# Probabilities times keys in three rounded passes, the high half kept by ScalarE and the low half by VectorE

## What is computed

```python
x = _layernorm(x + attention(x))                  # linear: A = sum(l2norm(K) * V); Y = A * l2norm(Q)
x = _layernorm(x + cross_attention(ctx, x))       # below
x = _layernorm(x + experts(x))                    # 8 experts, the best 2 of each row

def cross_attention(image, latents):              # image = ctx, latents = x; 16 heads of width 64
    kv_in = concat([norm(image), norm(latents)])  # 128 rows of keys per sequence
    w = softmax((norm(latents) @ Wq) * (kv_in @ Wk) / 8)
    return (w @ (kv_in @ Wv)) @ Wo
```

## Time and profile before

| | us |
|---|---|
| median of three runs | 1611.88 (1607.72 to 1613.25) |
| the profiled execution, whole | 1606.26 |
| its span, first to last instruction | 1604.4 |
| TensorE busy | 1432.5 (89%) |
| VectorE busy | 1105.5 (69%) |
| ScalarE busy | 1031.7 (64%) |
| GpSimd busy | 904.7 (56%) |

### The profile page before, as it was taken

One profiled execution on the slowest core, in us unless ns is written; L12 is line 12 of the kernel. 1 busy time (PEld: TensorE's weight loads), 2 busy tenths in 40 slices (PEclk: granted clock), 3 DMA queues, 4 the chain that ended last, 5 costly groups with the idle time before them and its releaser, 6 DMA issues.

```text
span 1604.4 us, 36488 instructions
## 1 busy us (share of the span) xinstructions
PE 1432.5 (89%) x10509; PEld 1239.7 (77%) x10509; DVE 1105.5 (69%) x4107; ACT 1031.7 (64%) x3827; POOL 904.7 (56%) x1233
## 2 busy tenths in 40 slices
PE   5699999999999999999999999999997499999940
PEld 4578888888888888888888888888886498889940
DVE  3366777767777677776777767777666588777865
ACT  2377776777767777677776777767764255555535
POOL 3355556665566665666556665566544255455565
PEclk9799999999999999999999999999999699999975
DMA  2000000000000000000000000000000676677746
GB/s 78 11 11 8 15 16 15 18 16 15 16 15 18 17 14 16 15 18 17 14 16 15 17 17 14 16 16 17 10 10 14 181 242 218 213 221 225 222 153 196
DMA packets 64624, 96.18 MB, mean 60 GB/s; under 512 B 10892, under 2 KB 48786, under 8 KB 64306
## 3 DMA queue, kind: packets, MB, share of 16 engines
q1 hardware_dynamic: 44738, 71.90, 15.0%
q0 software_dynamic: 8896, 16.94, 3.1%
q10 hardware_dynamic: 10800, 5.06, 1.2%
HBM read 71.55 MB, written 23.35 MB: 59 GB/s over the span
## 4 chain that ended last, share of the span: by engine, by line
PE 69%; DVE 10%; ACT 9%; DMA 4%; issue 4%; POOL 2%; SPq 2%; ACTq 0%; POOLq 0%; DVEq 0%
PE ps_s L1208 15%; PE ps_o L1221 11%; PE ps_t L1241 10%; ACT probs L607 6%; PE ps_pT L1231 5%; PE ps_t L1371 3%; PE ps_u L1256 3%; PE ps_a L1307 3%; PE ps_u L1258 3%; PE ps_u L1257 3%; DVE neg_max L759 3%; DVE pT L771 3%; PE ps_u L1371 2%; DVE k_pick L814 2%; DMA f_x<-x_rows 2%
## 5 line engine op out<-in xcount | busy, mean ns | idle before, releaser
L607 ACT ACTIVATE probs<-ps_s,neg_max 128x128 f32<-128x128 f32 x1024 | 361.8, 366 | 290.2 <-DVE neg_max L759 290.2
L496 POOL TENSOR_TENSOR probs_n<-probs,inv_sum 128x512 f32<-128x512 f32 x256 | 265.9, 1039 | 251.6 <-DVE inv_sum L765 249.6
L1208 PE MATMUL ps_s<-kvT,u_sb 128*128 128x128 f32 x2048 | 281.1, 280 | 0.0
L1208 PEld LDWEIGHTS ps_s<-kvT,u_sb 128*128 128x128 f32 x2048 | 255.2, 192 | 33.2 <-issue 31.8
L1241 PE MATMUL ps_t<-pT,kv_rows 128*128 128x512 f32 x512 | 262.2, 594 | 0.8 <-DVE pT L771 0.8
L1221 PE MATMUL ps_o<-value_w,tT 128*128 128x128 f32 x2048 | 260.5, 275 | 2.4 <-ACT tT L618 2.2
L759 DVE TENSOR_REDUCE neg_max<-ps_s 128x4 f32<-128x512 f32 x256 | 176.2, 688 | 103.9 <-PE ps_s L1208 103.4
L1221 PEld LDWEIGHTS ps_o<-value_w,tT 128*128 128x128 f32 x2048 | 244.0, 192 | 4.3 <-ACT tT L618 4.3
L553 POOL DMA_INDIRECT y_rows<-wvT,f_id x144 | 144.8, 1006 | 152.4 <-DVE wvT L1118 94.9
L607 ACT ACTIVATION_READ_ACCUMULATOR probs<-ps_s,neg_max 128x1 f32 x1024 | 208.2, 203 | 0.0
L508 POOL DMA_INDIRECT x_rows<-routed,pos_i x128 | 136.7, 1068 | 121.2 <-DVE pos_i L950 101.0
(11 more groups left out here) (237 smaller groups left out, 3165.6 us busy)
## 6 DMA issues: line engine op xcount, KB each, us to landing
u_sb<-in_expert_w SPq DMA_DIRECT2D x45, 578.0 KB
tT<-in_expert_w SPq DMA_DIRECT2D x27, 578.0 KB
f_x<-x_rows SPq DMA_DIRECT2D x72, 130.0 KB
tT<-y_rows SPq DMA_DIRECT2D x16, 512.0 KB, 4.7
x_raw<-in_x SPq DMA_DIRECT2D x64, 64.0 KB, 1.8
c_raw<-in_ctx_in SPq DMA_DIRECT2D x64, 64.0 KB, 2.0
out<-u_sb ACTq DMA_DIRECT2D x16, 256.0 KB, 2.4
y_rows<-wvT,f_id POOLq DMA_INDIRECT x144
```

The costliest lines, as they stand in the source:

```text
L496: nc.gpsimd.tensor_tensor(probs_n[:, sl], probs[:, sl], inv_sum[:, sl, :].rearrange("p (u o) -> p u o", o=1).to_broadcast([P, UP, P]), ALU ...
L607: last = nc.scalar.activation(probs[:, sl, j], ps_s[sl][:, j * P:(j + 1) * P], ACT.Exp, bias=neg_max[:, sl, j:j + 1], accum_out=sums[:, sl ...
L1208: last = nc.tensor.matmul(ps_s[sl][:, j * P:(j + 1) * P], u_sb[:, c // 2, BT * p + b, h:h + 2].rearrange("p h s -> p (h s)"), kvT[:, c, 2 ...
```

## The change

The key rows and the transposed probabilities are each kept as a rounded high half and the float32r rest: kv_hi, kv_lo, pT_hi, pT_lo. weigh becomes three rounded passes of 512 columns into the same bank: high x high, low x high, high x low; the third waits for pT_lo. ScalarE writes pT_hi (`round_pT`, behind the copy of u in each unit) and kv_hi; VectorE writes pT_lo = ps_pT - pT_hi (`keep_pT`, now of unit n-2, directly behind row_max(n)) and kv_lo (`rows_low`, in unit 2). turn_probs waits for pT_lo_done in place of pT_done, and at k = 1 and 3 stands behind latents_part in place of ahead of it; two small products wait for kv_lo_done in place of kv_done.

```diff
-        kv_rows = sb("kv_rows", [P, KV_RING, BT, D])
+        kv_hi = sb("kv_hi", [P, KV_RING, BT, D], F32R)
+        kv_lo = sb("kv_lo", [P, KV_RING, BT, D], F32R)
...
-        pT = sb("pT", [P, 2, UP * P])
+        pT_hi = sb("pT_hi", [P, 2, UP * P], F32R)
+        pT_lo = sb("pT_lo", [P, 2, UP * P], F32R)
...
+            def round_pT(t, k):
+                m, ss = t * 4 + (k - 1), (k - 1) % 2
+                act.wait_ge(pT_ps, m + 1)
+                act.wait_ge(t_ps, count(m - 1))
+                nc.scalar.activation(pT_hi[:, ss], ps_pT[:], ACT.Copy).then_inc(pT_hi_done, 1)
...
                         nc.scalar.activation(u_sb[...], ps_u[...], ACT.Copy).then_inc(u_done, 1)
+                    if unit_on(t, k - 1):
+                        round_pT(t, k)
...
-                        nc.scalar.activation(kv_rows[:, (t + 2) % KV_RING], KV_BACK..., ACT.Copy).then_inc(kv_done, 1)
+                        nc.scalar.activation(kv_hi[:, (t + 2) % KV_RING], KV_BACK..., ACT.Copy).then_inc(kv_hi_done, 1)
...
                 def keep_pT(k):
-                    m, ss = t * 4 + (k - 1), (k - 1) % 2
-                    dve.wait_ge(pT_ps, m + 1)
-                    dve.wait_ge(t_ps, count(m - 1))
-                    nc.vector.tensor_copy(pT[:, ss], ps_pT[:]).then_inc(pT_done, 1)
+                    m, ss = t * 4 + (k - 2), k % 2
+                    dve.wait_ge(pT_hi_done, m + 1)
+                    nc.vector.tensor_tensor(pT_lo[:, ss], ps_pT[:], pT_hi[:, ss].bitcast(F32), ALU.subtract).then_inc(pT_lo_done, 1)
...
+                def rows_low():
+                    dve.wait_ge(kv_hi_done, t + 3)
+                    nc.vector.tensor_tensor(kv_lo[...], KV_BACK..., kv_hi[...].bitcast(F32), ALU.subtract).then_inc(kv_lo_done, 1)
...
                 if on(t, 0):
                     row_max(0)
+                if unit_on(t, -2):
+                    keep_pT(0)
...
                 if on(t, 0):
                     inverse_sum(0)
-                if unit_on(t, -1):
-                    keep_pT(0)
...
                 if on(t, 0):
                     row_max(2)
+                if unit_on(t, 0):
+                    keep_pT(2)
+                if on(t, 2):
+                    rows_low()
...
             def turn_probs(t, k):
-                pe.wait_ge(pT_done, m)
+                pe.wait_ge(pT_lo_done, m)
...
             def weigh(t, k, p):
-                pe.wait_ge(pT_done, m + 1)
-                pe.wait_ge(kv_done, m // 4 + 1)
+                pe.wait_ge(pT_hi_done, m + 1)
+                pe.wait_ge(kv_lo_done, m // 4 + 1)
                 pe.wait_ge(t_done, m)
-                nc.tensor.matmul(ps_t[:], kv_rows[:, m // 4 % KV_RING, b], pT[:, ss], start=True, stop=True).then_inc(t_ps, 1)
+                nc.tensor.matmul(ps_t[:], kv_hi[:, own, b], pT_hi[:, ss], start=True, stop=False)
+                nc.tensor.matmul(ps_t[:], kv_lo[:, own, b], pT_hi[:, ss], start=False, stop=False)
+                pe.wait_ge(pT_lo_done, m + 1)
+                nc.tensor.matmul(ps_t[:], kv_hi[:, own, b], pT_lo[:, ss], start=False, stop=True).then_inc(t_ps, 1)
...
-                    if unit_on(t, k - 1):
+                    if k % 2 == 0 and unit_on(t, k - 1):
                         turn_probs(t, k)
...
                         if k != 2 and pair_on(t, p):
                             latents_part(t, k, c)
+                        if k != 2 and unit_on(t, k - 1):
+                            turn_probs(t, k)
```

More of the change, by code:

```diff
@@ L271, in decoder_layer @@
         neg_top_done g_lat_set kv_ps z1_done z1_stats z1_moments z1_eps z1_rstd x1_done l_hat_done
-        kv_done kvT_ps kvT_done lT_done upper_done score_split u_ps u_done s_ps max_done exp_done inv_done p_done pT_ps pT_done
+        kv_hi_done kv_lo_done kvT_ps kvT_done lT_done upper_done score_split u_ps u_done s_ps max_done exp_done inv_done p_done pT_ps pT_hi_done pT_lo_done
         t_ps t_done o_ps z2_done z2_stats z2_moments z2_eps z2_rstd x2_done
@@ L280, in decoder_layer @@
          neg_top_done, g_lat_set, kv_ps, z1_done, z1_stats, z1_moments, z1_eps, z1_rstd, x1_done, l_hat_done,
-         kv_done, kvT_ps, kvT_done, lT_done, upper_done, score_split, u_ps, u_done, s_ps, max_done, exp_done, inv_done,
-         p_done, pT_ps, pT_done, t_ps, t_done, o_ps, z2_done, z2_stats, z2_moments, z2_eps, z2_rstd,
+         kv_hi_done, kv_lo_done, kvT_ps, kvT_done, lT_done, upper_done, score_split, u_ps, u_done, s_ps, max_done, exp_done, inv_done,
+         p_done, pT_ps, pT_hi_done, pT_lo_done, t_ps, t_done, o_ps, z2_done, z2_stats, z2_moments, z2_eps, z2_rstd,
          x2_done, x2T_ps, x2T_done, gate_ps, logits_done, gexp_done,
@@ L669, in period @@
                         act.wait_ge(t_ps, count(4 * (t - 1)))
-                        nc.scalar.activation(kv_rows[:, (t + 2) % KV_RING], KV_BACK.rearrange("p (b d) -> p b d", b=BT),
-                                             ACT.Copy).then_inc(kv_done, 1)
+                        nc.scalar.activation(kv_hi[:, (t + 2) % KV_RING], KV_BACK.rearrange("p (b d) -> p b d", b=BT),
+                                             ACT.Copy).then_inc(kv_hi_done, 1)
             periods(act, period)
@@ L854, in split_latents @@
                                             ALU.subtract).then_inc(lT_done, 1)
+                def rows_low():
+                    dve.wait_ge(kv_hi_done, t + 3)
+                    nc.vector.tensor_tensor(kv_lo[:, (t + 2) % KV_RING], KV_BACK.rearrange("p (b d) -> p b d", b=BT),
+                                            kv_hi[:, (t + 2) % KV_RING].bitcast(F32), ALU.subtract).then_inc(kv_lo_done, 1)
                 def z2_sum():
@@ L988, in period @@
                     row_max(1)
+                if unit_on(t, -1):
+                    keep_pT(1)
                 if on(t, -3):
@@ L1022, in period @@
                     row_max(3)
+                if unit_on(t, 1):
+                    keep_pT(3)
                 if on(t, -3):
@@ L1237, in weigh @@
                 b = (k - 2) % 4 // 2
[L1238 to L1239 removed]
+                own = m // 4 % KV_RING
+                pe.wait_ge(pT_hi_done, m + 1)
+                pe.wait_ge(kv_lo_done, m // 4 + 1)
                 pe.wait_ge(t_done, m)
[L1241 removed]
+                nc.tensor.matmul(ps_t[:], kv_hi[:, own, b], pT_hi[:, ss], start=True, stop=False)
+                nc.tensor.matmul(ps_t[:], kv_lo[:, own, b], pT_hi[:, ss], start=False, stop=False)
+                pe.wait_ge(pT_lo_done, m + 1)
+                nc.tensor.matmul(ps_t[:], kv_hi[:, own, b], pT_lo[:, ss], start=False, stop=True).then_inc(t_ps, 1)
             def latents_part(t, k, c):
@@ L1296, in period @@
                         pe.wait_ge(logits_done, min(t - 2, NT))
-                        pe.wait_ge(kv_done, min(t + 3, NT))
+                        pe.wait_ge(kv_lo_done, min(t + 3, NT))
                         nc.tensor.matmul(B_RANK, ones[:], seen[:, p], start=True, stop=False)
```

6 lines of the change are left out of this document (removed).

## The result

The changed kernel takes 1651.1 us in the median of four runs (1645.12 to 1653.38), the kernel before, run beside it, 1609.8 (1605.24 to 1613.25): a ratio of 1.0267, 95% interval 1.024 to 1.0295. The forecast was 1650. So the change makes the kernel 2.7% slower. The same two kernels on another chip gave 1.0266 (1.0247 to 1.0284).

A forecast was written before the change was run, and what follows sets the result against it. The prediction took a loop through weigh(0)'s wait, TensorE's work to qkv and ScalarE's copies as the bound: 18.86 us per period against 18.22, 59 periods, 38 us on the median of 1611.9, so 1650 us, range 1624 to 1676.

The forecast's parts named there:

- The third pass: In weigh(0), it waits for pT_lo made behind row_max(0), takes about 0.49 us (0.38 to 0.60), ends at R+1.83.
- The idle of TensorE: Ahead of weigh(0)'s third pass: about 1.6 us, from the second pass's end at R-0.3 to R+1.34.
- The passes: The weighing of each unit: three rounded passes take 0.67 us (to 0.72) against 0.86, saving 0.75 per period.
- qkv: End of TensorE's qkv product, 10.11 us behind weigh(0)'s end: R+11.94.
- ScalarE: ScalarE's order behind the qkv product: free for exps(3) at qkv+2.40, last eviction ends at qkv+6.64.
- Rival 1: ScalarE's loop isn't the bound: 18.14 us per period, 1607 us, or 1600 with a third pass of 0.38; chance 0.14.
- The tile: From one row_max(0) to the next tile's: 18.86 us, against 18.22 in the kernel before.
- The moves forward: At the tile's end, keep_pT's removal from the chain and a shorter k_pick move kv_prod about 1.0 us forward.
- Units 1 to 3: There the wait for pT_lo is hidden behind 1.6 us or more of out and latent products.
- Rival 2: Costlier rounds, ScalarE copies or subtractions, or a lower clock: +0.3 to +0.7 us per period, 1668 to 1691; chance 0.15.
- Rival 3: At the tile's end kv_prod is held by GpSimd's scale(3): 18.71 us per period, 1641 us; chance 0.06 alone.
- The sum: 59 full periods at +0.64 us give 38 us; last four tiles set at 0, routed part untouched.

The follow-up runs named there:

- round3_last: The changed kernel with ScalarE's round_pT of unit 3 moved behind the three evictions: 18.44 us per tile, ratio 1.0104 to the kernel before.
- after: The changed kernel itself, as profiled, against the kernel before: 18.87 us per tile in place of 18.22, ratio 1.0267.
- lo0_first: The changed kernel with unit 0's subtraction (keep_pT) moved ahead of split_latents and row_max(0): 18.29 us per tile, ratio 1.0033 to the kernel before.
- weigh0_second: The changed kernel with weigh(0) moved behind the six latent products in TensorE's order: 18.17 us per tile, ratio 0.9992 to the kernel before.
- old_places: The kernel before with only keep_pT and turn_probs at their new places, plain product, no rounds: 19.53 and 21.15 us per tile, ratio 1.0729.
- lo0_route_place: lo0_route with three routing steps (place_picked, place_sum, place_int) moved into unit 2: 17.59 us per tile, ratio 0.9766 to the kernel before.
- changed_again: The changed kernel, unaltered, timed again on another chip beside the kernel before: 1649.28 us against 1607.75, ratio 1.0266.
- lo0_route: lo0_first with route_rows moved ahead of inverse_sum(0) on VectorE: 17.62 us per tile, ratio 0.9772 to the kernel before.

## Why the prediction was right

The loop that it named is the one that bounds, and its terms came out as follows (R is the start of row_max(0), 602.34; the qkv product ends at 614.40 in the same tile).

- **The third pass** was to end at R+1.83: it ended at R+1.84 (603.68 + 0.50). The lone pass was taken at 0.49 and measured 0.50. The 0.38 us that the Trainium skill (TensorE: Matmul & The Clock Gate, Single matmul latency) gives for a lone pass of 512 columns is stated for bf16; here a pass that stands behind another has a record of 0.39 to 0.40 (L1260 above), near that figure, and one behind a wait has 0.50, so the trace doesn't agree for the lone pass. The next instruction, however, started 0.34 us behind its start.
- **The idle of TensorE** was to be about 1.6: 1.51. The third pass started at R+1.34, as said; the second ended at R-0.17, not at R-0.3.
- **The passes** were taken as 0.67 (to 0.72) for three, and take 0.70.
- **qkv** was to end at R+11.94: R+12.06. Most of the 0.12 can be named: the one weighing inside took 0.70 in place of 0.67, the product 0.77 in place of 0.75, and the transposes of turn_probs ahead of it 0.49 in place of 0.44.
- **ScalarE** was to start exps(3) 2.40 behind that: 2.35, with no idle. Rival 1 didn't come: round3_last turned 0.48 us of ScalarE's order into 0.43 us of tile. TensorE alone would have allowed 18.14; in after score(0) ends at 620.42 (619.43 + 0.99 in the chain), which with 0.05 for the semaphore is 18.13 behind the R of this tile. But up to exps(3) ScalarE is the later by only 0.03 us (the prediction had 0.08), and no run tests the round of unit 2 alone: that its 0.48 us count is argued, not shown.
- **The tile** was to take 18.86: 18.87. The two small misses cancel.
- **The moves forward** came out as said: k_pick takes 0.20 in place of 0.63 and starts ahead of scale(3). **Units 1 to 3** show no wait for pT_lo, as said. So the sign followed from these: the wait of weigh(0), taken away alone, gives back 0.58 (lo0_first) or 0.70 (weigh0_second), one of the rounds alone 0.43, and both, or the wait with the held copy out of the way, bring the time under that of the kernel before.
- **Rival 2** didn't come: rounds cost 0.48, subtractions 0.68, and the clock stayed at 1.00 behind the idle of 1.51 us. But its ground was real: in old_places, with 1.73 us of idle, a lower clock did come.
- **Rival 3** had the rule right and the instruction wrong. kv_prod (618.53) started 0.06 us ahead of scale(3) (618.59) and took 0.28; the next product of two SBUF operands, pos_sel, came after it and was held till its end. The Trainium skill (SBUF — State Buffer, Who interferes with whom) has DVE instructions with two SBUF inputs contend with a GpSimd reader, and counts copies among those that can. The traces agree: pos_sel (1.01 us), mask in lo0_route_place (1.01), and the copy L946 in lo0_first (1.05). In after it costs nothing, for split_latents waits 0.46 for ScalarE anyway.

**The sum.** 59 tiles at +0.64 were to be 38 us. From the first tile's z1 (the sum that closes the first attention part, L841) to the last tile's it is 37.5 us more than before; this is the term. What was set at nothing was not. The last tiles, taken as even, cost 2.9 us (last z1 to the end of the routing). The experts and the norm, which the change doesn't touch, took 5.1 us more in this execution (362.8 in place of 357.7), and the part ahead of the first z1 0.6 less; the spans differ by 44.9. The same kernel in changed_again has 365.0 for the experts and the norm and lo0_route, on the same chip, 359.1, so this stretch moves by as much without the change; why stays open. The profiled execution was to be 1644 and was 1652.4. The forecast of 1650 was built on the median of the first three runs, 1611.9; against the 1609.8 of all four the time rose by 41.3 us, not 38. The two differences partly cancel in the total: its fit is in part luck, that of the tile is not.

## What to carry to other kernels

Before a new operand is made by a second engine, find the place in each engine's order at which it is first needed and the place at which it can first be made, and close the loop around a tile. Here TensorE had less to do and the time still rose by 2.7%, because one of four subtractions stood behind maxima that TensorE itself had still to feed, and because the rounds lengthened ScalarE's stretch in the same loop. With that subtraction ahead of the maxima and a two-column copy out of GpSimd's way, the same three passes are 2.3% faster than the kernel before.

## What the runs showed of the hardware

**A tiny VectorE instruction beside GpSimd.** A 128x2 integer copy (0.15 us) took 1.05 us beside GpSimd's 128x512 product, and 128x16 and 128x8 products (0.17 and 0.16) took 1.01: held to its end, whatever their size. One that started 0.06 us ahead of it wasn't slowed (0.28 us), and the GpSimd product behind it took 1.12 us in place of 1.04. When the held one was moved away, the next of its kind was held (lo0_route_place), so the thing to do is to see that nobody waits for the one that stands there: the same hold cost 0.67 us per tile at L946 and next to nothing at pos_sel.

**The clock and short idles.** In after 1.51 us of idle in nearly every tile left the granted clock at 1.00, and so did 1.78 us in one tile. With 1.73 us (old_places) it stayed in about two tiles of three and fell to 0.55, about the lower of its two levels (1.2 of 2.4 GHz), in the third, for some 3.6 us, which costs 1.6 us beside the idle itself. Rounded passes of 256 columns were 0.21 apart there in place of 0.12. The falls are not scattered: they come 2 or 5 tiles apart (40.7 or 99.3 us). Why one tile falls and its neighbour doesn't is open.

**Rounded passes of 512 columns** follow each other at 0.23 us and one behind a wait has a record of 0.50; a 128x512 ScalarE copy out of PSUM takes 0.47 to 0.50 of its engine's order whatever its record says (0.60 to 0.68, the longer ones beside GpSimd).
